# Two copies of the GELU rows, moved from ScalarE to VectorE

## What is computed

```
x = x + tanh(g_xattn) * xattn(layernorm(x), ctx, ctx)
x = x + tanh(g_ffn)   * ffn(layernorm(x))

xattn:  Q, K, V = linear projections;  qk = Q K^T
        feats per head = mean of scores, mean of row maxima, mean variance of softmax(qk / 4)
        t = exp(clip(w3 gelu(w2 gelu(w1 feats + b1) + b2) + b3))     # one temperature per batch and head
        out = softmax(qk / (2 t)) V, projected by Wo
ffn:    down(quant(silu(gate(quant(x))) * up(quant(x))))             # ternary weights, 8-bit activations
```

## Time and profile before

| | |
|---|---|
| median of 3 runs | 796.79 us (791.43 to 797.09) |
| the profiled execution | 792.8 us, span 791.0 us |
| PE busy | 702.7 us (89%) |
| DVE busy | 708.0 us (90%) |
| ACT busy | 683.9 us (86%) |
| POOL busy | 487.9 us (62%) |
| granted TensorE clock, mean | 0.962 |
| chain that ended last | PE 36%, ACT 35%, DVE 16%, issue 9% |

### The profile page before, as it was taken

One profiled execution on the slowest core, in us unless ns is written; L12 is line 12 of the kernel. 1 busy time (PEld: TensorE's weight loads), 2 busy tenths in 40 slices (PEclk: granted clock), 3 DMA queues, 4 the chain that ended last, 5 costly groups with the idle time before them and its releaser, 6 DMA issues.

```text
span 791.0 us, 20866 instructions
## 1 busy us (share of the span) xinstructions
PE 702.7 (89%) x7118; PEld 474.6 (60%) x7127; DVE 708.0 (90%) x1452; ACT 683.9 (86%) x1454; POOL 487.9 (62%) x956
## 2 busy tenths in 40 slices
PE   6567899999999999999999999999999888877896
PEld 4334566666666666667676766676765555533453
DVE  5779899989899999999999999899999776798995
ACT  1578899898999999999999999999999888768883
POOL 4747657667777667676766666767664043245663
PEclk9666899999999999999999999999999899999998
DMA  9997747464668575767455666656664122246688
GB/s 206 204 261 166 197 127 149 109 126 128 154 120 149 124 144 124 145 122 158 123 138 134 134 137 133 128 136 130 124 118 85 39 68 86 71 103 164 160 179 181
DMA packets 148887, 108.50 MB, mean 137 GB/s; under 512 B 56991, under 2 KB 145183, under 8 KB 148767
## 3 DMA queue, kind: packets, MB, share of 16 engines
q1 hardware_dynamic: 143630, 101.98, 58.3%
q10 hardware_dynamic: 5152, 5.19, 2.7%
HBM read 49.54 MB, written 12.85 MB: 79 GB/s over the span
## 4 chain that ended last, share of the span: by engine, by line
PE 36%; ACT 35%; DVE 16%; issue 9%; DMA 2%; ACTq 1%; POOL 1%; SPq 0%; DVEq 0%; POOLq 0%
ACT ex L1197 13%; ACT pt L1187 12%; PE p_o L1348 7%; PE p_m L1426 6%; PE p_s L1328 5%; PE p_m L1407 5%; PE p_t L1369 4%; DVE kst L1032 3%; DVE hmax L1035 3%; PE p_m L1415 3%; ACT L1223 3%; ACT L1187 2%; DVE stats L907 2%; PE p_m L1399 2%; DVE nm L926 2%
## 5 line engine op out<-in xcount | busy, mean ns | idle before, releaser
L1197 ACT ACTIVATE ex<-p_s,nm 112x375 f32<-112x375 f32 x512 | 275.8, 618 | 12.3 <-DVE nm L926 11.0
L1187 ACT ACTIVATE pt<-p_t,ct 128x336 f32<-128x336 f32 x488 | 245.8, 577 | 26.7 <-PE p_t L1369 24.5
L907 DVE BATCH_NORM_STATS2 stats<-ex 112x6 f32<-112x375 f32 x512 | 252.5, 535 | 1.4 <-ACT ex L1197 1.3
L926 DVE TENSOR_REDUCE nm<-p_s 112x2 f32<-112x750 f32 x256 | 236.0, 922 | 1.2 <-PE p_s L1328 1.0
L1328 PE MATMUL p_s<-kst,qst 96*112 96x375 bf16 x512 | 154.8, 348 | 13.5 <-ACT ex L1197 7.3
L1369 PE MATMUL p_t<-qst,kst 99*128 99x112 bf16 x1464 | 115.1, 213 | 4.9 <-ACT pt L1187 4.0
L1369 PEld LDWEIGHTS p_t<-qst,kst 99*128 99x128 bf16 x1464 | 91.1, 98 | 44.0 <-issue 19.7
L1407 PE MATMUL p_m<-wv_sb,ctxt 128*128 128x256 f32 (+1 forms) x384 | 106.7, 401 | 4.7 <-DVE va L859 2.9
L1348 PE MATMUL p_o<-pt,va 128*32 128x112 f32 (+1 forms) x3072 | 101.7, 265 | 1.4 <-ACT pt L1187 0.8
L1426 PE MATMUL p_m<-ctxt,wk_sb 128*128 128x375 f32 x240 | 94.6, 518 | 1.7 <-DVE qf L875 1.1
L1328 PEld LDWEIGHTS p_s<-kst,qst 96*112 96x112 bf16 x512 | 67.0, 139 | 45.7 <-ACT ex L1197 34.6
(11 more groups left out here) (187 smaller groups left out, 1164.3 us busy)
## 6 DMA issues: line engine op xcount, KB each, us to landing
kst<-kp SPq DMA_DIRECT2D x378, 93.8 KB, 3.5
ctxt<-ctxt_dram SPq DMA_DIRECT2D x32, 375.0 KB, 4.2
qbounce<-qp SPq DMA_DIRECT2D x32, 168.0 KB, 2.5
qst<-qbounce SPq DMA_DIRECT2D x32, 168.0 KB, 3.6
qst<-qbounce SPq DMA_DIRECT2D x32, 112.0 KB, 3.4
xm<-x_dram SPq DMA_DIRECT2D x32, 112.0 KB, 2.4
x_dram<-x SPq DMA_DIRECT2D x32, 112.0 KB, 1.9
xt<-x_dram SPq DMA_DIRECT2D x28, 128.0 KB, 3.2
```

What stands on the lines that cost most here:

```text
L907: last = nc.vector.bn_stats(stats[:, nb % RING, 2 * pb + i], ex[0:SQ, 2 * (t % 2) + i, :])
L926: nc.vector.tensor_reduce(nm[:, n % RING, 2 * p:2 * p + 2], p_s[t % 2][0:SQ, :, 0:SK], axis=AX.X, op=ALU.max, negate=True).then_inc(s_max, 1)
L1187: nc.scalar.activation(pt[:, (2 * r + i) % 8], st_home(r, i)[:, 0:KC * SQ].rearrange("k (c q) -> k c q", c=KC), ACT.Exp, scale=ct[:, nr % ...
L1197: nc.scalar.activation(ex[0:SQ, 2 * ((t - 1) % 2) + i, :], p_s[(t - 1) % 2][0:SQ, i, 0:SK], ACT.Exp, bias=nm[:, ne % RING, h:h + 1]).then_ ...
```

## The change

The predicate `with_gelu(n)` is true for even rows n from 2 * 26 // 8 = 6 to 30. In those rows DVE executes the copy of the weighted sums (slot 4, behind `x2` and before a small reciprocal, `fa`) and that of the second key piece (slot 5, in front of everything that DVE does in that slot). ACT leaves both out there. The key copy exists where the batch n + 2 exists, so in rows 6 to 28. The semaphores and their counts are the same.

```diff
+        def with_gelu(n):
+
+            return pair_of(n) and 2 * BACK // SLOTS <= n < B
...
 (DVE, slot)
+                if p == 4 and 0 <= m < B and with_gelu(n):
+
+                    dve.wait_ge(s_pv, count(4, m, 4))
+                    if m > 0:
+                        dve.wait_ge(s_ob, count(1, m))
+                    nc.vector.tensor_copy(oa[:, :, :], o_acc).then_inc(s_oc, 1)
+                if p == 5 and 0 <= n + K_AHEAD < B and with_gelu(n):
+
+                    f = n + K_AHEAD
+                    dve.wait_ge(s_kmm, count(2, f, 2))
+                    dve.wait_ge(s_kp2, count(2, f - 1, 2))
+                    nc.vector.tensor_scalar(kf[:, 1], p_m[:, 0:SK], bk[:, 1:2], 0.0, ALU.add, ALU.add,
+                                            accum_out=sumk[:, f % SRING, 1:2]).then_inc(s_kc, 1)
...
 (ACT, slot)
-                copying = p in (3, 5) and 0 <= f < B
+                copying = p in (3, 5) and 0 <= f < B and not (p == 5 and with_gelu(n))
...
-                if p == 4 and 0 <= m < B:
+                if p == 4 and 0 <= m < B and not with_gelu(n):
```

## The result

The changed kernel is a little slower: 799.17 us (median of 16 runs) against 793.62 us (16 runs of before beside it), ratio 1.0066 with a 95% interval of 1.0046 to 1.0087, so +5.2 us (3.7 to 6.9; the two medians differ by 5.5). The forecast was slower by 7.6 us, 804 us on a median of 796.8, range 795 to 812.

What follows compares the result with a forecast made beforehand. PE's queue, then ACT's, was taken as the chain in each pair of rows. DVE's lateness, 8 x 0.785 + 3 x 0.455 = 7.6 us, on the median of 796.8 gave 804 us, range 795 to 812.

Steps and rivals of the forecast that it cites:

- ACT's relief: Slots 4 and 5 of even rows: ACT loses 0.98 us of copies, worth nothing because PE's queue is the chain.
- The wait of 1.19 us: DVE's slot 7 wait for the third V matmul; looks like spare room, but the shared bank p_m leaves 0.13 us.
- The path through the second V copy: Slot 7: late DVE delays the second V copy, so the third V matmul starts 0.905 us late, ACT's exponentials 0.785.
- The room: Lateness absorbed by slot 7: DVE's wait 0.10 us before the second V copy, 0.13 before the third V matmul, ACT's 0.12.
- The accumulator read: Reading the key sum on DVE behind the key copy: unknown, taken as 0.15 us, bounds 0 and 0.36.
- The slip of the transposes back: PE's transposes back need DVE's key copy, ending at about 306.0, so PE and the GELU slip 0.2 us.
- Row 30: Only the sums' copy moves there, 0.53 us, of which at most 0.18 would remain; left out of the sum.
- Absorbed: Rival: DVE's 1.19 us wait before the third V copy takes all the added work; 0 us, 796.8 us, chance 0.10.
- ACT-bound: Rival: ACT's queue sets slots 4 and 5 of even rows; 10.8 us less, 786.0 us, chance 0.06.
- Longer DVE instructions: Rival: each instruction added on DVE holds the queue for its duration less 0.27 us more; +14.3 us, chance 0.08.
- The sum's own band: The 7.6 us sum over 11 pairs with the accumulator read at its bounds: 6.0 to 10.0 us slower.

Runs made afterwards that it cites:

- e4: Kernel before, ACT's two copies cut to one column each, no key sum, nothing added on DVE; rows 8 to 29 418.1 us, ratio 0.9978.
- e5: Kernel before, ACT's copies kept, two unused bn_stats of 448 elements added on DVE where the change has its copies; rows 8 to 29 423.4 us, ratio 1.0054.
- e1: Changed kernel with the key copy back on ACT, only the sums' copy on DVE; rows 8 to 29 418.7 us, ratio to before 0.9982.
- e2: Changed kernel with the sums' copy back on ACT, only the key copy on DVE; rows 8 to 29 418.6 us, ratio to before 0.9982.
- e6: Changed kernel plus a third DVE load, a bn_stats of 448 elements in slot 5; rows 8 to 29 429.9 us, ratio to before 1.0136.
- e3: Changed kernel with DVE's second V copy before the tile statistics in slot 7; rows 8 to 29 420.4 us, ratio to before 1.0043.
- e11: Kernel before with only DVE's second V copy put before the tile statistics in slot 7; rows 8 to 29 417.7 us, ratio 0.9999.
- e9: As e3, with DVE's key copy also moved from slot 5 into slot 4; rows 8 to 29 418.2 us, ratio to before 0.9965.
- e7: Changed kernel's sums' copy on DVE in odd rows from 7 instead of even ones, key copy not moved; rows 8 to 29 423.2 us, ratio 1.0022.

## Why the prediction was right, and what was mis-sized

- *ACT's relief is worth nothing.* Shown by e4 (418.1) and by the equality of e5 and the changed kernel.
- *The wait of 1.19 us is not room.* Shown: it is still 1.06 after the change and in e1, e2, e5 and e6, while the pairs grow by 0.07 to 1.11. It shrinks (to 0.47 in e3 and e11, 0.34 in e9) only where the statistics move into it.
- *The path through the second V copy.* Shown by e3 (0.37 of the 0.57 us go away), the kink of e1, e2 and the change, and the full slope of e6.
- *The room.* The term was too small. I subtracted DVE's idle 0.10 before the second V copy. But an instruction that need not wait starts 0.08 before the end of the one in front, so the room there was 0.18. With 0.18, 0.13 and 0.12 the threshold is 0.43, and e1's 0.53 leaves 0.10 (measured 0.07).
- *The accumulator read.* Taken as 0.15 us, it costs nothing: the read lies beside the next instruction. The main instruction takes 0.597 us instead of 0.535, so the key copy holds the queue for 0.52, where I had 0.605.
- With these two: 1.05 - 0.43 = 0.62 in eight pairs and 1.05 - 0.51 - 0.25 = 0.29 in three, 5.8 us, against 5.4 in the trace and 7.6 forecast. The last 0.04 to 0.05 a pair I can't name.
- *The slip of the transposes back,* 0.2, was right (0.21). In rows 8 to 29 it is hidden behind the larger one, as forecast; e3 uncovers it, and e9 shows that it is the key copy's. In row 6 it isn't hidden: the row costs 0.22 (21.96 to 22.18), where the forecast had nothing. It stays in e3 (22.17) and is gone in e1, e2 and e5 (21.96 to 21.97), where the key copy is not late.
- *Row 30,* left out at "at most 0.18": 19.68 against 19.55 to 19.56 in e4 and e9, +0.12 to 0.13. With row 6 that is 0.3 us outside rows 8 to 29.
- *Rivals.* Absorbed (0.10): wrong, though either half alone is nearly absorbed. ACT-bound (0.06): wrong, by e4. Longer DVE instructions (0.08): wrong, the next instruction starts 0.08 before the end of the new copies as behind the bn_stats. The drain of the Trainium skill (VectorE: DVE Perf Modes, section The DRAIN you can't avoid) doesn't show here either. The prediction gave only half of what that section says: it adds that a next instruction that is not held starts earlier, and the 0.08 agree with that.
- *The range and the medians.* The baseline was 793.6 over 16 runs, not the 796.8 of three; that took 3 us off the time and nothing off the ratio. The sum's own band, 6.0 to 10.0 us, was missed: 5.2 and 5.4 lie under it, because its lower end allowed for a free accumulator read but not for the larger room. That 799 lies in the range of 795 to 812 is thus in part luck of the baseline and of a wide range; the mechanism does not rest on it.

## What to carry to other kernels

A long wait on an engine is room only if what it waits for does not itself wait for that engine's previous instruction; look one step back, at the buffer that both share. Two moves that are nearly free alone can be dear together: the room is a threshold, so price a change by the sum of what is late there. And before moving work off the engine that the chain names, compare at each hand-over when the others arrive: where two come within hundredths, relieving one gains nothing, and an order that puts the copy that PE needs before work that nobody waits for is what makes room.

## What was not expected of the hardware

- A tensor_scalar with a sum on DVE runs as two instructions, 0.597 us for 375 elements from PSUM (a bn_stats of 375 takes 0.535) and a read of 0.080 us which starts together with the next instruction. On ACT the read (0.24 us) holds the queue for 0.09.
- The program does not fix the time to better than some microseconds: stretches of 3 to 4 us at a granted clock of 0.50 (1.2 GHz) turned up in different rows in different executions (row 30 before, row 7 after and in five of the experiments, row 20 in e6, row 12 in e7), each costing 0.6 to 1.5 us. PE had waited shortly ahead of those four (for ACT 0.59 and 0.23 us in row 7 after, 1.23 in row 30 before, 1.12 in row 12 of e7; for DVE 1.06 in row 20 of e6), but other even rows have the like without a fall; what sets it off stays open.
